# A four-layer graph network on one core: SAGE units made between the sweeps of the layer before, batches of edges from high destinations, and three shifts in the order of work

## What is computed

```python
x = _layernorm(x + L0(x, edges, edge_weight))   # three GCN layers with weights and self loops, then Wl
x = _layernorm(x + L1(x, src, dst))             # two SAGE layers: x @ W_self + mean_agg(x) @ W_neigh + b
x = _layernorm(x + L2(x, edges))                # encoder, five GRU steps on segment_sum((h @ w)[src], dst), decoder
x = _layernorm(x + L3(x, edges))                # one GCN layer with counts and self loops
```

## Time and profile before

| what | us |
|---|---|
| median of 3 runs | 5464.75 (5461.94 to 5466.56) |
| the profiled execution | 5469.89 |
| its span, first to last instruction | 5467.3 |
| TensorE busy | 4736.8 (87%) |
| GpSimd busy | 2486.2 (45%) |
| VectorE busy | 1805.1 (33%) |
| ScalarE busy | 1189.7 (22%) |
| mean granted clock of TensorE | 0.910 |

### The profile page before, as it was taken

The page is one execution under the profiler, slowest core; times in us unless marked ns, Lnnn a source line. Parts: engine busy times, 40 slices in busy tenths (PEclk is TensorE's granted clock), DMA queues, the critical chain, the costliest instruction groups (busy, mean ns, idle before and its releaser), DMA issues. The chain is left out here.

```text
span 5467.3 us, 77806 instructions
## 1 busy us (share of the span) xinstructions
PE 4736.8 (87%) x25659; PEld 2547.9 (47%) x25659; DVE 1805.1 (33%) x3217; ACT 1189.7 (22%) x2478; POOL 2486.2 (45%) x1708
## 2 busy tenths in 40 slices
PE   3544544499899999999998999899999999999999
PEld 3544444444344444444453544444444444444444
DVE  9999999910001000110050201302113031130642
ACT  4555555411011111111120101202112021120320
POOL 5888888888888888888888000000000000000000
PEclk7555555599999999999999999999999999999999
DMA  9999993399899999999988786595775857768477
GB/s 355 367 365 338 340 312 54 31 319 283 255 287 296 279 299 288 295 277 299 281 237 234 249 280 223 167 299 183 250 248 183 299 177 256 239 192 298 143 229 249
DMA packets 717675, 1402.14 MB, mean 256 GB/s; under 512 B 268948, under 2 KB 356840, under 8 KB 692456
## 3 DMA queue, kind: packets, MB, share of 16 engines
q1 hardware_dynamic: 477388, 1342.89, 73.5%
q0 software_dynamic: 225792, 0.70, 7.9%
q10 hardware_dynamic: 14364, 56.99, 2.8%
HBM read 1160.09 MB, written 240.26 MB: 256 GB/s over the span
## 5 line engine op out<-in xcount | busy, mean ns | idle before, releaser
L877 PE MATMUL psum<-arena 128*128 128x512 f16 (+3 forms) x14014 | 3665.3, 423 | 70.8 <-DMA arena<-C_adj 31.8
L877 PEld LDWEIGHTS psum<-arena 128*128 (+2 forms) x14014 | 1668.0, 123 | 2006.0 <-issue 924.8
L572 POOL DMA_INDIRECT W_adj<-arena x784 | 1214.0, 1548 | 278.9 <-issue 246.9
L572 POOL DMA_INDIRECT C_adj<-arena x784 | 1217.3, 1553 | 247.0 <-issue 247.0
L727 POOL TENSOR_TENSOR arena<-arena 128x512 f32 (+1 forms) x13 | 21.8, 1678 | 1716.1 <-DVE arena L1275 1716.1
L442 DVE TENSOR_SCALAR_CACHE_REDUCE arena<-arena 128x2048 bf16<-128x2048 f32 (+7 forms) x392 | 709.1, 1873 | 0.0
L520 PE MATMUL psum<-arena 128*128 (+1 forms) x6664 | 211.2, 167 | 561.9 <-DVE arena L467 335.9
L520 PEld LDWEIGHTS psum<-arena 128*128 128x128 bf16 x6664 | 207.0, 104 | 570.2 <-issue 516.7
L1471 DVE COPY arena<-psum 128x512 f32<-128x512 f32 (+1 forms) x39 | 23.2, 654 | 1139.7 <-PE psum L895 1139.7
L274 ACT ACTIVATE arena<-arena 128x1024 bf16<-128x1024 f32 (+7 forms) x392 | 298.4, 773 | 453.8 <-DVE arena L480 271.9
L1473 DVE TENSOR_SCALAR arena<-psum,arena 128x512 f32<-128x512 f32 x30 | 21.9, 748 | 1038.9 <-PE psum L877 1038.9
(11 more groups left out here) (238 smaller groups left out, 2575.0 us busy)
## 6 DMA issues: line engine op xcount, KB each, us to landing
arena<-C_adj SPq DMA_DIRECT2D x784, 384.0 KB, 3.8
arena<-W_adj SPq DMA_DIRECT2D x294, 768.0 KB, 4.3
arena<-C_adj SPq DMA_DIRECT2D x392, 512.0 KB, 4.5
arena<-W_adj SPq DMA_DIRECT2D x147, 1024.0 KB, 5.2
arena<-C_adj SPq DMA_DIRECT2D x392, 288.0 KB, 3.7
arena<-W_adj SPq DMA_DIRECT2D x147, 576.0 KB, 4.8
W_adj<-arena SPq DMA_DIRECT2D x12, 6400.0 KB
W_adj<-arena SPq DMA_DIRECT2D x12, 6144.0 KB
```

What stands on the lines that cost most here:

```text
L572: return pool.indirect_dma_start(table, bass.IndirectOffsetOnAxis(idx[:, t:t + 1], 0), values[:, of:of + 1], None, compute_op=ALU.add)
L877: ins = pe.matmul(psum[:, bank + b, 0:width], lhs, ring[:, slot, b * BANK:b * BANK + width], start=begin and part == 0, stop=False, skip_g ...
```

## The change

- `ORDER` is reversed, so batches come from high destinations; the padding edges move from the last batch to the end of batch 0; blocks are zeroed from the highest down, and `zones` counts from there.
- The stages start and gcn 2 sweep downwards: blocks 9 to 12, 5 to 8, 1 to 4, and 0 alone (`DOWNWARD`).
- `DVE_ROWS` is 6 instead of 8: ScalarE does rows 6 to 15.
- The dense part of sage 0 is taken out of its stage. While a sweep of gcn 2 runs, the SAGE units of the sweep before are made: products and transposes between laps of eight chunks, the units of blocks 1 to 4 all together ahead of the last sweep, and unit 0 inside the first sweep of sage 0, which starts at chunk 4. The results lie in `sum_fm` and `h_fm`, and the splitting into `h_parts` (`two_parts`) is done when stage gcn 2 is over.
- The first unit of each gru stage and of out is made inside the last sweep of the stage before (`head`): products after two laps, transposes after four.
- In enc the chunks lag by two (`ENC_LAG`), and one of them stands ahead of the products.

```diff
+ORDER = ORDER[::-1]
-DVE_ROWS = TB // 2
+DVE_ROWS = 6
+DOWNWARD = ((9, 4, 0), (5, 4, 4), (1, 4, 0), (0, 1, 4))
+ENC_LAG = 2
+SAGE_BANKS = ((0, 1, 2), (4, 5, 6), (5, 6, 7), (5, 6, 7))
...
-            for z in range(BLOCKS):
+            for done, z in enumerate(reversed(range(BLOCKS))):
...
+            dve.wait_ge(s["late_rows"], b * (TB - DVE_ROWS) + half - DVE_ROWS)
...
-            if k:
+            if k and name != "sage":
                 pe.wait_ge(s["dve_stage"], k)
                 pe.wait_ge(s["act_stage"], k)
...
+            def sage_products(j, sweep, ahead):
+                n = sage_units().index(j)
+                pe.wait_ge(s["products_read"], ahead.read + n)
+                near, own, _ = SAGE_BANKS[sweep]
+                for c in range(UC):
+                    sl, nodes_ = slice(c * D, (c + 1) * D), slice(j * BANK + c * P, j * BANK + (c + 1) * P)
+                    pe.matmul(psum[:, own, sl], h_fm[:, nodes_], wt["W1s"], start=True, stop=True)
+                    ins = pe.matmul(psum[:, near, sl], sum_fm[:, nodes_], wt["W1n"], start=True, stop=True)
+                ins.then_inc(s["products"], 1)
+            def sage_turned(j, sweep, ahead, before):
+                n = sage_units().index(j)
+                pe.wait_ge(s["seconds_read"], ahead.seconds + n)
+                pe.wait_ge(s["unit_set"], before + n + 1)
+                for c in range(UC):
+                    ins = pe.transpose(psum[:, SAGE_BANKS[sweep][2], c * P:(c + 1) * P],
+                                       sum_fm[:, j * BANK + c * P:j * BANK + (c + 1) * P], ident)
+                ins.then_inc(s["seconds"], 1)
...
-                spell((j - 1) * UC)
                 seconds(j, q)
-                spell((j - 1) * UC + 1)
+                spell((j - 1) * UC - ENC_LAG + 1)
...
+                    if early and sweep == SPLIT:
+                        pe.wait_ge(s["sum_dve"], base.sum_dve)
+                        pe.wait_ge(s["sum_act"], base.sum_act)
...
+                        for j in sage_units_of(sweep - 1):
+                            sage_products(j, sweep - 1, ahead)
+                            sage_turned(j, sweep - 1, ahead, before)
                     chunk(0, LAP, sweep, 16 * (base.sweep + 1), True)
...
+                    if sweep == SPLIT and headed(stages, k + 1):
+                        for lap in range(HEAD_LAPS):
+                            if lap == 2:
+                                pe.wait_ge(s["sum_dve"], base.sum_dve)
+                                pe.wait_ge(s["sum_act"], base.sum_act)
+                                pe.wait_ge(s["kept"], kept_before(stages, k + 1))
+                                gate_products(0, HEAD_BANKS)
+                                last_gate(0, HEAD_BANKS[3])
```

More of the change, by code:

```diff
@@ L84, in walk, with walk_on @@
     with eng.Fori(0, (UNITS - 1) // 2) as i:
+        for q in (1, 0):
+            j = 2 * i + (2 - q)
+            lead(j, q)
+            after(2 * i + (1 - q), 1 - q)
+            main(j, q)
+    after(UNITS - 1, 0)
+def walk_on(eng, lead, main, after):
+    lead(1, 1)
+    main(1, 1)
+    lead(2, 0)
+    after(1, 1)
+    main(2, 0)
+    with eng.Fori(1, (UNITS - 1) // 2) as i:
         for q in (1, 0):
@@ L594, in last_layer, with sweeps_of, sage_units, sage_units_of @@
     return last
+def sweeps_of(name, arg):
+    return DOWNWARD if (name, arg) in (("start", None), ("gcn", 2)) else SWEEPS
+def sage_units():
+    return [j for sweep in range(len(DOWNWARD)) for j in range(DOWNWARD[sweep][0], sum(DOWNWARD[sweep][:2]))]
+def sage_units_of(sweep):
+    first, n, _ = DOWNWARD[sweep]
+    return range(first, first + n)
+def sage_splits():
+    return [j for j in range(UNITS) if j not in sage_units_of(SPLIT)] + list(sage_units_of(SPLIT))
+def sage_chunk(place):
+    return (place + SAGE_FIRST) % CHUNKS
+def headed(stages, k):
+    return k < len(stages) and stages[k][0] in ("gru", "out")
+def bases_before(stages, k):
+    base = Bases()
+    for stage in stages[:k]:
+        base.advance(*stage)
+    return base
+def kept_before(stages, k):
+    return 1 + UNITS * sum(((n, a) in (("gcn", 2), ("enc", 1)) or n == "gru") for n, a, _ in stages[:k])
 def blocks_of(sweep):
@@ L745, in sync @@
             wide_before = wide
-            for sweep, (first, n, _) in enumerate(SWEEPS):
+            for sweep, (first, n, _) in enumerate(sweeps_of(name, arg)):
                 c0 = first * BANK
@@ L762, in sync @@
                         sp.wait_ge(added[u], least[u])
+                if (name, sweep) == ("sage", 0):
+                    load(sage_chunk(0), LAP)
+                    with sp.Fori(0, LAPS - 1) as i:
+                        for u in range(LAP):
+                            sp.wait_ge(s["chunk_used"], i * LAP + (used + u - LAP + 2))
+                            load(i * LAP + (u + 1 + SAGE_FIRST), u)
+                    for u in range(LAP):
+                        place = (LAPS - 1) * LAP + u + 1
+                        sp.wait_ge(s["chunk_used"], used + place - LAP + 1)
+                        load(sage_chunk(place), u)
+                    used += CHUNKS
+                    continue
                 load(0, LAP)
@@ L1191, in scalar @@
                             last_unit(j)
+                    if sweep == SPLIT and headed(stages, k + 1):
+                        head(bases_before(stages, k + 1), stages[k + 1][0])
+                    if (name, arg) == ("gcn", 2) and sweep:
+                        for j in sage_units_of(sweep - 1):
+                            sage_kept(j, sweep - 1, bases_before(stages, k + 1))
                     if not wide:
@@ L1257, in vector @@
             base_units, base_new = units_before(stages, k), new_before(stages, k)
[L1258 to L1259 removed]
+            kept = kept_before(stages, k)
             dve.wait_ge(s["kept"], kept)
@@ L1300, in two_parts, with sage_unit @@
                                          op1=ALU.subtract).then_inc(s["features_set"], 1)
-                dve.wait_ge(s["features_set"], j + (base.features + 1))
+                dve.wait_ge(s["features_set"], (j if n is None else n) + (base.features + 1))
+            def sage_unit(j, sweep, ahead, before):
+                n = sage_units().index(j)
+                dve.wait_ge(s["products"], ahead.products + n + 1)
+                near, own, _ = (bank_nm(b) for b in SAGE_BANKS[sweep])
+                for c in range(UC):
+                    ins = dve.scalar_tensor_tensor(out=work[:, c, :], in0=near[:, c, :],
+                                                   scalar=rdeg[:, j * UC + c:j * UC + c + 1], in1=row["sb1"],
+                                                   op0=ALU.mult, op1=ALU.add)
+                link(ins)
+                dve.tensor_tensor(work, work, own, ALU.add).then_inc(s["products_read"], 1)
+                dve.wait_ge(s["products_read"], ahead.read + n + 1)
+                dve.tensor_scalar(sum_nodes(j), work, 0.0, None, ALU.max).then_inc(s["unit_set"], 1)
+                dve.wait_ge(s["unit_set"], before + n + 1)
             def out_free(j, seconds_of=True, kept_of=True):
@@ L1416, in vector @@
             else:
-                with step.loop(0, (UNITS - 1) // 2, 2 * per) as i:
+                if headed(stages, k):
+                    main(1, 1)
+                    after(1, 1)
+                    main(2, 0)
+                with step.loop(1 if headed(stages, k) else 0, (UNITS - 1) // 2, 2 * per) as i:
                     for q in (1, 0):
@@ L1460, in vector @@
                             last_unit(j)
+                    if sweep == SPLIT and headed(stages, k + 1):
+                        head(bases_before(stages, k + 1), stages[k + 1][0])
+                    if (name, arg) == ("gcn", 2) and sweep:
+                        for j in sage_units_of(sweep - 1):
+                            sage_unit(j, sweep - 1, bases_before(stages, k + 1), units_before(stages, k + 1))
                     base.used += CHUNKS
```

222 lines of the change are left out of this document (162 added, 60 removed).

## The result

| what | before | after |
|---|---|---|
| median, us | 5464.4 (5461.9 to 5466.6, 4 runs) | 5420.5 (5415.6 to 5428.5, 4 runs) |
| ratio, 95% interval | | 0.9924 [0.9912, 0.9937] |
| span of the profiled execution, us | 5467.3 | 5420.8 |
| build over, TensorE's first chunk | 1108.1 | 986.8 |
| stage start over | 1659.0 | 1619.1 |

The kernel became 44 us faster; 60 was forecast (5405, range 5383 to 5428). The stage times are read from the traces, at the border that VectorE reports. They say where it fell short: behind the SAGE stage 40.0 us were gained (2107.4 to 2067.4), where the prediction had 35; up to its end 6.5 us, where it had 25.

The account below looks back on a forecast made before the run. Two chains, TensorE's and GpSimd's, with GpSimd's adds the later one at 3014 us and TensorE bounding nearly every stage after the build. Gains of 25 + 18 + 15.5 + 1.8 = 60 us gave 5405 us, range 5383 to 5428.

Parts of the forecast that it names:

- What bounds the kernel: Before 3014 us, where gcn 2's last sweep waits for C_adj, an edit counts only through GpSimd's chain of adds.
- The build: Build stage: two compare rows moved from VectorE to ScalarE gain some 128 us, which doesn't reach the end.
- the rival on ScalarE: Build: ScalarE's burst bounds it once a batch takes over 22.9 us; at 24 us the time is 5519; chance 0.04.
- The order of the batches: GpSimd's adds: reversed batches and zeroing make the last C add 22 us later, at about 3030.
- the same pair in the C phase: GpSimd's C adds: two successive batches share a destination; the wait for landing was taken as 2 us, against 6 beside zeroing.
- Does TensorE get there in time?: Ahead of gcn 2's last sweep: TensorE arrives at 2997 and waits 39 us; with no build gain, at about 3030.
- The one-block sweep: Gcn 2's last sweep: SyncE's issue of 49 loads makes it about 31 us, ending at 3067.5.
- the rival of 42 us: Gcn 2's one-block sweep is slow, 42 to 47 us instead of 31, giving 5416 to 5421; chance 0.15.
- SAGE: First SAGE layer: twelve of 13 units leave, 262 us stay of 290.3, after a wait of about 2 us.
- Encoder, GRU, out: Later stages: filled TensorE waits gain 18 us in the encoder, 15.5 at GRU boundaries and 1.8 in the output stage.
- the first term: Everything up to the end of the first SAGE layer: 25 us gained, ending at 3331.5 against 3356.4.
- GpSimd loses more at the start: Narrow-block zeroing is slower than its size, or a landing beside it takes 25 us: about 5423; chance 0.10.

Follow-up runs that it names:

- rows8: The changed kernel with VectorE doing eight compare rows again instead of six; 5412.7 us, ratio 0.9895.
- throttle: The changed kernel with SyncE holding loads back in sweep 1 of start too, until the one three places earlier has landed; 5408.4 us, ratio 0.9896.
- order_only: The kernel before with only the reversed batches, zeroing from the highest block and downward sweeps; 5474.3 us, ratio 1.0017.
- throttle_gcn: The changed kernel with SyncE holding loads back in sweep 1 of start and in gcn 0's first sweep; 5403.5 us, ratio 0.9886.
- static_issue: The changed kernel with the 48 loads behind the first of gcn 2's one-block sweep written out instead of looped; 5421.5 us, ratio 0.9917.
- enc_back: The changed kernel with the encoder's chunks back in their places, no lag and none ahead of the products; 5450.1 us, ratio 0.9968.
- no_head: The changed kernel with the first unit of each gru stage and of out made in its own stage again; 5442.2 us, ratio 0.9962.
- order2_static_throttle: The changed kernel with batches 48, 47, 45, 43, 46 first, one-block sweep loads written out, and loads held back in sweep 1 of start; 5388.6 us, ratio 0.9856.

## Why the prediction was right, and where its size was off

**What bounds the kernel.** Right, and more strongly than written. GpSimd's adds end last ahead of gcn 2's last sweep, the build gain of 121 us (128 forecast) is covered by two waits of TensorE of 88.8 and 38.2 us, and it comes out below nothing: rows8, without it, is 8 us faster. This sign the prediction did not see. Its text says that an edit ahead of 3014 counts only through GpSimd, but then lets the faster build touch GpSimd nowhere.

**The build.** 121 us against 128: 2.5 us a batch instead of 2.7, and ScalarE, busy 16.9 us a batch (810.5 / 48) where a burst of 17.2 was worked out, didn't bound it. In the rival on ScalarE the threshold is added up wrongly: with the 6 us of the prediction it is 21.5 + 6/48 = 21.6 us and not 22.9, and by its own terms TensorE had nothing to spare (3047 against 3036). It doesn't matter here, since a batch took 19.1 us (916 / 48).

**The order of the batches: the mis-sized term.** The forecast was 22 us, measured were 39. Batch by batch, in us later than before: 18 at the second batch of W (14 forecast); 25 at the third (20 forecast; the pair's 6.65 was as taken); from there the usual pauses brought it to 22, by their lengths here and there; 30 behind the pause at 1144; 44 behind the landing at 1641; 39 at the end, the kernel before having its own longer pauses. Some 3 of these us are at the very start: the first add comes at 71.8 here and at 68.3 to 68.5 in the three kernels with this order and eight rows on VectorE (in throttle, with six rows, at 70.6). GpSimd waits there for the zeroed blocks; why they are later with six rows no run shows. The step that failed is "I take 6 ... and 2 for the same pair in the C phase, where it is over": 13.9 us in place of 2. And the sum has no term for a recurring pause that grows: at 1144 it grew from 3.7 to 11.6. The prediction looked for what else is on the queues by the *old* times, where at 1627 a last sweep of start was running. With stage start 40 us earlier gcn 0's load burst stood there. The order alone (order_only) makes 21.3 us; the meeting of bursts and adds makes most of the rest, as throttle and throttle_gcn show by taking it away at either place (the last C add falls from 39.1 us later than before to 25.8); the 4.4 us that stay are the 3 of the start and the chance of the pauses.

**Does TensorE get there in time?** Yes, at 3014 instead of 2997. Twelve of these 17 us were there at the end of start (1619.1 against 1607), from W's adds, which ended at 1567.9 and not 1558. The rest is that each of the four units made one by one takes 6.2 to 7.1 us and not 5.2; rows8, where they bound, shows it. It cost nothing here.

**The one-block sweep.** 31 us forecast, 32.4 measured. The forecast counted one turn of SyncE's loop at 1.1 us; there are five, and between them a load each 0.60. The granted clock over the sweep is 0.94, a mean of two parts. Windows of its first 4.1 us and of the stretch from 3060 on:

```profile
3052.36:3056.50 4.14, 3.95 (x11) 1.19 (x12) 0.00 (x0) 0.00 (x0) 0.00 (x0) 0.56 0.76 215
...
3060.00:3084.80 24.80, 21.59 (x77) 7.26 (x76) 0.00 (x0) 0.00 (x0) 0.00 (x0) 1.00 0.73 203
```

In the wait of 38 us the clock was 0.50, that is 1.2 GHz, and it stayed there for most of the first 4 us; from then on it was 2.4 GHz to the end, at 87% busy with pauses of 0.2 to 0.5 us. By the Trainium skill ("TensorE: Matmul & The Clock Gate", A second HAM failure mode) such pauses can make the clock swing; here, behind the first 4 us, they didn't, and the rival of 42 us falls. That the issue is the bound is shown by static_issue. The 138 GB/s that the skill gives for 64 KB ("DMA: Bandwidth & Descriptors", Bandwidth), by which this was an estimated 47 us, is no measure for this row of loads, issued from SyncE with several in flight: the sweep moved its 128 KB loads at 203 GB/s, and at 254 when they were issued closer together.

**SAGE.** 263.5 us against 262, after a wait of 1.6 (2 forecast). Right.

**Encoder, GRU, out.** 18 forecast, 18.4 by the run without it. 15.5 and 1.8 forecast for the units ahead, 17.3 together by the run without them. Both were read off waits in rows of before and filled with work that had to be done anyway, and that they came out so close has some luck in it, as the same stage differs by up to 3.4 us between kernels. The 40.0 us behind the SAGE stage are 4.3 more than these two make. By the stage times 2.3 of them lie in enc (enc_back without its GRU unit against before), 1.5 in the gru stages and 0.5 in out (no_head against before). What gives them isn't settled; they are little more than the 3.4 us by which one such stage differs anyway.

**Sum.** 25 + 18 + 15.5 + 1.8 = 60 became 6.5 + 40.0 = 46.5 between the profiled spans, 44 in the medians. Of the 18.5 us lost in the first term 16 to 17 are GpSimd's lateness, 1.4 the sweep and 1.5 the SAGE stage, with some tenths gained at the borders. The time lies inside the range because the rival "GpSimd loses more at the start" reached to it (5423), though with its cause at the wrong place: it happened at 1144 and 1627 us, not beside the zeroing. That the range holds the time is to that extent luck.

## What to carry to other kernels

When an edit brings a stage forward, redraw what runs beside it at the new times, for the engine that bounds above all: here an engine off the path became faster, its loads started earlier, and they slowed the adds on the path. A part whose price is a lateness is to be measured alone as well as together, since 21 us alone became 39 with the rest. Filling a wait of known length with the next piece of the same work was the safest gain to forecast here; and loads that were needed late could be held to a few in flight beside GpSimd's adds, which paid with 12 us in throttle and 8 in order2_static_throttle.

## What the runs showed of the hardware

- A stream of GpSimd's indirect DMAs, written out without a loop, pauses between two instructions once in 112 adds. In the thirteen profiles the pause is up to 7.2 us of idleness on most occasions (at 933 in the changed kernel there is none) and 11 to 20 beside a burst of 1 MB loads: 11.6, 12.3, 14.6, 17.0, 18.6 and 20.0 at the same add in six kernels, 11.0 at another add in rows8; 2.6, 3.2 and 4.2 at that add with the loads held back. The Trainium skill ("Runtime: NRT & Kernel Launch", Instruction fetch mechanics) says that an engine refills its instructions in blocks of 256 by a DMA of its own, and that crossing a block is "mostly hidden". The regular distance and the growth with the queued loads would fit such a refill that isn't hidden here. But the trace lists no packet of the kind "instruction" between 1142 and 1156 (it may not record them all), and a batch has 26 recorded instructions on GpSimd in the W phase and 21 in the C phase, while the distance is 112 adds in both. So something that goes by the number of adds is as open, and what the pause is isn't shown.
- The landing of an add's last bytes, as GpSimd waits for it ahead of the next batch, was 2.9 to 4.6 us without a burst beside it (4.6 with loads held back), 6.4 to 8.4 beside the zeroing and 13.4 to 15.4 beside the burst.
- SyncE issues a small load each 0.60 us inside its loop, with 1.1 at each turn of it (eight loads), and each 0.47 us when the loads are written out.
- TensorE's granted clock was 0.50 in a wait of 38 us and about that for the first 4 us behind it, and then 1.00 for the rest of a sweep that was 87% busy with many pauses of 0.2 to 0.5 us.
